# A ternary image layer: where its activations are scaled, rounded and searched for their maximum

## The reference

```python
def bitnet_linear(x, W, b):
    w_scale = jnp.maximum(jnp.mean(jnp.abs(W)), 1e-05)
    qW = jnp.sign(W) * (jnp.abs(W) > 0.5 * w_scale).astype(W.dtype)
    i_scale = jnp.maximum(jnp.max(jnp.abs(x)), 1e-08) / 127.0
    qx = jnp.clip(jnp.round(x / i_scale), -128.0, 127.0)
    out = jnp.einsum('...i,oi->...o', qx, qW) * (w_scale * i_scale)
    return out + b
vis = bitnet_linear(dinov2_features, W_d2v, b_d2v)
image_embeds = bitnet_linear(vis, W_img, b_img)
fused = bitnet_linear(text_embeddings, W_txt, b_txt)
for Wa, ba in ((W_att0, b_att0), (W_att1, b_att1)):
    kv = bitnet_linear(image_embeds, Wa, ba)
    k = jnp.concatenate([kv, kv], axis=-1)
    scores = jnp.einsum('bse,bpe->bsp', fused, k) * inv_sqrt_e
    attn = jax.nn.softmax(scores, axis=-1)
    fused = fused + 0.1 * jnp.einsum('bsp,bpe->bse', attn, k)
avg_img = jnp.mean(image_embeds, axis=1, keepdims=True)
concatenated = jnp.concatenate([fused, jnp.broadcast_to(avg_img, (b, s, e))], axis=-1)
h = jax.nn.relu(bitnet_linear(concatenated, W_f1, b_f1))
return bitnet_linear(h, W_f2, b_f2)
```

## Time and profile before

| | us |
|---|---|
| median of 3 runs (2675.1 to 2678.14) | 2677.37 |
| the profiled execution | 2671.04 |
| its span | 2669.1 |
| PE busy in the span (share) | 2413.4 (90%) |
| DVE busy (share) | 1359.3 (51%) |
| ACT busy (share) | 931.5 (35%) |
| ternary layer, from its first DMA issue to the next layer's | 1712.8 to 2111.9 |

### The profile page before, as it was taken

How to read it: one execution, slowest core, us unless ns; L and a number is a source line. 1 busy time by engine, 2 the same in 40 slices (tenths; PEclk the granted TensorE clock), 3 DMA queues, 4 the chain that set the end, 5 groups by cost and what they waited for, 6 DMA issues and landing times. The chain is left out here.

```text
span 2669.1 us, 31308 instructions
## 1 busy us (share of the span) xinstructions
PE 2413.4 (90%) x11901; PEld 1244.3 (47%) x11901; DVE 1359.3 (51%) x1929; ACT 931.5 (35%) x1903; POOL 650.8 (24%) x538
## 2 busy tenths in 40 slices
PE   7899999899999999878699799886988679999997
PEld 4454444344555555445445454354665323333332
DVE  5799999315788876630545412385444511111114
ACT  3677676025433335201122110285333212222221
POOL 0489888100000000010211000000000033444442
PEclk9999999999999999989789899998998789999998
DMA  3632222555344445315600100202000252460534
GB/s 106 250 97 92 92 86 85 125 202 207 112 169 162 163 118 171 134 53 212 213 0 0 44 1 3 97 1 95 1 1 4 103 209 100 200 279 27 234 112 158
DMA packets 97066, 301.29 MB, mean 113 GB/s; under 512 B 27114, under 2 KB 57990, under 8 KB 82332
## 3 DMA queue, kind: packets, MB, share of 16 engines
q1 hardware_dynamic: 63264, 171.06, 19.1%
q0 software_dynamic: 33664, 128.35, 13.1%
HBM read 446.13 MB, written 47.22 MB: 185 GB/s over the span
## 5 line engine op out<-in xcount | busy, mean ns | idle before, releaser
L1064 PE MATMUL psum<-at_Wv,at_context 128*128 128x512 f32 (+1 forms) x576 | 265.0, 599 | 0.0
L837 PE MATMUL psum<-mb_context,mb_key_w 128*128 128x361 f32 x768 | 252.4, 478 | 11.4 <-PEq L894 6.2
L778 DVE TENSOR_TENSOR_SCAN ms_state<-ms_decay,psum 128x800 f32<-128x800 f32 x128 | 233.0, 1820 | 6.1 <-DVE psum L775 1.7
L3134 ACT ACTIVATE tf_hidden<-psum,tf_b 128x64 f32<-128x64 f32 x512 | 108.2, 362 | 363.9 <-PE psum L3091 338.9
L3102 PE MATMUL psum<-tf_W,tf_hidden 128*64 128x512 f32 x1024 | 228.1, 597 | 3.9 <-ACT tf_hidden L3134 2.4
L3080 PE MATMUL psum<-tf_W,tf_x_T 128*64 128x512 f32 x1024 | 228.7, 597 | 1.7 <-issue 0.8
L837 PEld LDWEIGHTS psum<-mb_context,mb_key_w 128*128 128x128 f32 x768 | 141.5, 191 | 126.3 <-issue 31.5
L810 POOL TENSOR_TENSOR x_rows<-ms_state,mb_C_everywhere 128x800 f32<-128x800 f32 x86 | 161.9, 1886 | 102.7 <-DVE ms_state L778 86.5
L1165 ACT ACTIVATE mb_weights_and_rows<-psum,at_neg_max 100x722 f32<-100x722 f32 x128 | 110.4, 862 | 143.1 <-DVE at_neg_max L1227 142.9
L3015 POOL DMA_INDIRECT tf_W<-in_L_W,tt_weight_row x120 | 119.5, 996 | 164.2 <-PE psum L3080 116.6
L1227 DVE TENSOR_REDUCE at_neg_max<-psum 100x1 f32<-100x722 f32 x128 | 115.5, 903 | 78.1 <-PE psum L1085 77.7
(11 more groups left out here) (489 smaller groups left out, 3802.6 us busy)
## 6 DMA issues: line engine op xcount, KB each, us to landing
at_piece<-in_L_W_f POOLq DMA_DIRECT2D x24, 1024.0 KB, 5.9
keys_dram<-x_rows SPq DMA_DIRECT2D x128, 180.5 KB, 1.9
mb_key_w<-keys_dram SPq DMA_DIRECT2D x64, 361.0 KB, 3.2
sf_W<-in_L_W SPq DMA_DIRECT2D x16, 1024.0 KB, 7.0
tf_W<-in_L_W SPq DMA_DIRECT2D x8, 2048.0 KB, 20.9
mb_context<-in_ctxT SPq DMA_DIRECT2D x16, 541.5 KB, 4.4
at_context<-in_ctxT SPq DMA_DIRECT2D x8, 1083.0 KB, 4.9
ternary_dram<-at_piece_made POOLq DMA_DIRECT2D x14, 512.0 KB
```

Source lines behind the costliest of these rows:

```text
L778: nc.vector.tensor_tensor_scan(state[:, n % RH, :], decay[:, g % RA, :, :].rearrange("p b l -> p (b l)"), drive, 0.0, ALU.mult, ALU.add).t ...
L837: last = nc.tensor.matmul(side("key", u, t == KE - 1)[:, 0:SH], lhsT=wk[:, k, e * P:(e + 1) * P], rhs=keys[:, h, k, :], start=(k == 0), st ...
L1064: last = nc.tensor.matmul(bank[0:rows_of(t), :], lhsT=ctxT[:, b % 2, k, t * P:t * P + rows_of(t)], rhs=wv[:, k, h * BANK:(h + 1) * BANK], ...
```

## The change

Five edits. (1) Scales, bias, `d2v` weights and the first vision chunk get buffers of their own (`FirstSeen`), loaded by SyncE during the feed-forward's last product; the text maximum is taken there too, batch by batch. (2) `see` and `bl_img` become one block; the last chunk's maximum is taken in four pieces; the chain's TensorE steps stand between text units; the first chunk is rounded in halves; ScalarE's scalings stand between its drains. (3) `bl_emb` is gone: its chain stands at the start of `ternary_attend`, and VectorE scales and rounds the image embeddings there, half a chunk at a time (`quantise`), the first two chunks before the attention and the other six inside it. The weights of the last products are loaded in two parts when chunks 4 and 6 have been rounded, as they take their place. (4) `joint_linear`: the maxima over `x_cols` are taken in the odd phases of the attention, ScalarE rounds the means, VectorE rounds the first half of the text before it scales the second; the last hidden maxima are taken unit by unit. (5) In the output layer VectorE scales half of the first batch. All large buffers lie in one tensor, `tn_space`.

The cut diff:

```diff
+            for b in range(NB if most is not None else 0):
+                dve.wait_ge(turned.done(b), turned.n + b + 1)
+                nc.vector.tensor_reduce(most[:, b:b + 1], c.xT[:, :, b * L:(b + 1) * L], mybir.AxisListType.XY, ALU.max,
+                                        apply_absolute_value=True)
...
+    def load(self, sp):
+        c = self.c
+        sp.dma_start(self.scales[:, :], c.scales[:, :]).then_inc(self.loaded, 16)
+        sp.dma_start(self.w[:, :, :], made_ternary(c, "d2v")).then_inc(self.loaded, 16)
+        sp.dma_start(self.rows[:, :, :], c.vision[0].rearrange("p (k s) -> p k s", k=KC)).then_inc(self.loaded, 16)
+        sp.dma_start(self.bias[:, :], c.dram["L1_bias_cols"]).then_inc(self.loaded, 16)
...
+        TURN_AT, GIVE_AT = 4, 5
+        BY_SCALAR = {3: (5, 0), 6: (5, 1), 9: (6, 0), 12: (6, 1), 15: (7, 0), 18: (7, 1)}
...
             for v, (h, f) in enumerate(x_units):
-                u = len(units) + v
+                if v == TURN_AT:
+                    i_top.turn(pe)
+                if v == GIVE_AT:
+                    i_top.give(pe)
+                u = N + v
...
+            for f in range(KD):
+                prod.wait_free(pe, N + NX + f)
+            for h in range(2):
+                pe.wait_ge(i_rounded, h + 1)
+                for f in range(KD):
+                    last = image_half(f, 0, f, h)
+                    if h:
+                        last.then_inc(prod.filled, 1)
+            for v, (b, f) in enumerate(units):
+                if b == 0:
+                    continue
+                if f == 0:
+                    pe.wait_ge(i_rounded, b + 2)
+                prod.wait_free(pe, N + NX + v)
+                for h in range(2):
+                    last = image_half(v, b, f, h)
+                last.then_inc(prod.filled, 1)
...
+            for v, (b, f) in enumerate(units):
+                u = N + NX + v
+                prod.wait_full(act, u)
+                nc.scalar.activation(wide[:, b, f, :].rearrange("p (z s) -> p z s", s=SH), prod.bank(u), ACT.Identity,
+                                     scale=i_oscale[:, :], bias=bias_of("img")(f), accum_out=sums[:, f, b:b + 1]).then_inc(prod.done(u), 1)
+                if v in BY_SCALAR:
+                    z, h = BY_SCALAR[v]
+                    nc.scalar.activation(wide[:, z, :, part(h)], wide[:, z, :, part(h)], ACT.Copy,
+                                         scale=i_top.inv[:, :], bias=MAGIC).then_inc(i_scaled_s, 1)
...
+                for f in range(KD) if b == NB - 1 else (None,):
+                    largest(b, f, 0).then_inc(seen_most, 1)
+            dve.wait_ge(seen_most, NB - 1 + KD)
+            i_top.start(dve, amax[:, :])
+            i_top.finish(dve)
+            nc.vector.tensor_tensor(i_oscale[:, :], i_top.scale[:, :], one_scale("img"), ALU.mult).then_inc(i_scale_ready, 1)
+            dve.wait_ge(i_top.inv_ready, 1)
+            def scale(at, n):
+                nc.vector.tensor_scalar(at, at, i_top.inv[:, :], MAGIC, ALU.mult, ALU.add).then_inc(i_scaled, 1)
+                dve.wait_ge(i_scaled, n)
+            def spread(dst, at):
+                nc.vector.tensor_scalar(dst, at, MAGIC, None, ALU.subtract).then_inc(i_rounded, 1)
+            for h in range(2):
+                scale(wide[:, 0, :, part(h)], h + 1)
+                spread(seen(0, h), wide[:, 0, :, part(h)])
+            whole = lambda b: image[:, :, b * S:(b + 1) * S]
+            for b in range(1, 4):
+                scale(wide[:, b, :, :], b + 2)
+                spread(whole(b), wide[:, b, :, :])
+            largest(0, None, N + NX)
+            scale(wide[:, 4, :, :], 6)
+            spread(whole(4), wide[:, 4, :, :])
+            for b in range(5, NB):
+                dve.wait_ge(i_scaled_s, 2 * (b - 4))
+                spread(whole(b), wide[:, b, :, :])
...
+            top.start(dve, cmax[:, :])
+            top.finish(dve)
+            nc.vector.tensor_tensor(oscale[:, :], top.scale[:, :], wscale, ALU.mult).then_inc(oscale_ready, 1)
+            dve.wait_ge(top.inv_ready, 1)
+            for z in range(2):
+                nc.vector.tensor_scalar(c.xT[:, :, half(z)], c.xT[:, :, half(z)], top.inv[:, :], MAGIC, ALU.mult, ALU.add).then_inc(scaled, 1)
+                dve.wait_ge(scaled, z + 1)
+                nc.vector.tensor_scalar(catq[:, 0:KD, half(z)], c.xT[:, :, half(z)], MAGIC, None, ALU.subtract).then_inc(rounded, 1)
...
+            for lo, hi, b in f_parts:
+                sp.wait_ge(e_rounded, 2 * b + 2)
+                sp.dma_start(wf[:, lo:hi], c.ternary[:, c.ternary.shape[1] - F_ALL + lo:c.ternary.shape[1] - F_ALL + hi]).then_inc(f_loaded, 16)
...
+            def quantise(b, z):
+                if b >= NB:
+                    return
+                at = wide[:, b, :, part(z)]
+                nc.vector.tensor_scalar(at, at, e_top.inv[:, :], MAGIC, ALU.mult, ALU.add).then_inc(e_scaled, 1)
+                dve.wait_ge(e_scaled, 2 * b + z + 1)
+                nc.vector.tensor_scalar(seen(b, z), at, MAGIC, None, ALU.subtract).then_inc(e_rounded, 1)
+            e_top.start(dve, amax[:, :])
+            e_top.finish(dve)
             at0 = TERNARY.index("att0")
-            nc.vector.tensor_scalar(kscale[:, :], wscale[:, at0:at0 + 2], iscale[:, :], None, ALU.mult).then_inc(scale_ready, 1)
+            nc.vector.tensor_scalar(kscale[:, :], wscale[:, at0:at0 + 2], e_top.scale[:, :], None, ALU.mult).then_inc(scale_ready, 1)
+            dve.wait_ge(e_top.inv_ready, 1)
+            for b in range(2):
+                for z in range(2):
+                    quantise(b, z)
             nc.vector.memset(prob[:, :, S:], 0.0).then_inc(cleared, 1)
             nc.vector.memset(kr[64:P, :, :, ST - 1, :], 0.0).then_inc(cleared, 1)
+            for s in range(2):
+                query(0, s)
             dve.wait_ge(cleared, 2)
             ringR.grant(dve)
-            for s in range(2):
-                query(0, s)
-            take_rows(0, range(NR))
+            take_rows(0, range(4))
+            quantise(2, 0)
+            take_rows(0, range(4, 8))
+            quantise(2, 1)
+            take_rows(0, range(8, NR))
+            own(nc.vector.tensor_scalar(sums[:, :, :], sums[:, :, :], 1.0 / S, None, ALU.mult))
+            own(nc.vector.tensor_reduce(cmax[:, NB:], sums[:, :, :], mybir.AxisListType.XY, ALU.max, apply_absolute_value=True))
...
                     take_rows(f + 1, range(2, 4) if s == 0 else range(4, 9))
+                quantise(f + 3, 0)
+                quantise(f + 3, 1)
...
+                    else:
+                        b = f // 2 * 2 + s
+                        nc.vector.tensor_reduce(cmax[:, b:b + 1], c.xT[:, :, b * L:(b + 1) * L], mybir.AxisListType.XY, ALU.max,
+                                                apply_absolute_value=True)
```

408 lines of the change are left out of this document (207 added, 201 removed).

## The result

The changed kernel takes 2643.62 us (median of 4 runs, 2639.63 to 2648.33), the kernel before, run beside it on the same chip, 2676.23 (4 runs): ratio 0.9883, 95% interval [0.9867, 0.9898]. In the first experiment, the changed kernel again, it was 2641.02 (6 runs) against 2673.31 (8 runs): 0.9895 [0.9877, 0.9913]. The ratios are estimates of their own and not the quotients of the medians, which are 0.9878 and 0.9879.

The account below looks back on a forecast made before the run. TensorE bounds the attention, VectorE the stretches between stages. Gains of 2.7 + 3.3 + 15.3 + 4.7 + 2.4 = 28.4 us take the profiled 2671.04 to 2642.6, and the median, 6.3 above, to 2649.0; range 2642 to 2662.

Parts of the forecast that it names:

- the sum: Ternary layer: gains of 2.7, 3.3, 15.3, 4.7 and 2.4 us over five steps, 28.4 in all.
- First loads: Layer's start: four loads moved ahead, first vision matmul sooner, with VectorE's eight text maxima setting it; gain 2.7 us.
- Merged stage: Vision and image product in one block: text tail and boundary go, VectorE sets the end; gain 3.3 us.
- Rival B: Merged stage: ScalarE is the bound, drains at 1.28 plus half scalings; loss of 2.8 there, 2655 us; chance 10 in 100.
- Quantising in the attention: Image maximum's end to turning of keys: 12.5 us instead of 27.7, remaining chunks scaled inside the attention; gain 15.3.
- The cover: Attention phases: VectorE's waits for TensorE hide its halves, costed at nothing; without it 3.4 us in each of five phases.
- Rival A: Attention: VectorE is late, all ten halves uncovered, 17 us lost, 2666; half of them, 2657; chance 12 in 100.
- its neighbour: VectorE's halves run at one element a cycle, 3.2 us; gain 10, 2667; chance 3 in 100.
- The margin: Attention phases: 3.4 us of VectorE's halves fit into its 3.46 wait before the first addition, leaving 0.06.
- Joint layer's start: Attention's end to first joint matmul: 4.6 us instead of 9.26, without the maximum over the columns; gain 4.7.
- Output: Output layer: last maximum over 400 elements saves 1.25 us, first row scaled by two engines 1.2; gain 2.4.
- Rival C: Attention phases: waits for VectorE's halves keep TensorE at the lower clock, 7.7 us a phase, up to 2710; chance 2 in 100.

Follow-up runs that it names:

- three edits together: Changed kernel with text maximum cut in three, ScalarE's half scalings earlier, and chunk 1 scaled by ScalarE at the attention's start: 2633.55 us, ratio 0.9875.
- the kernel with three roundings more: Changed kernel with each half of chunks 3 to 7 rounded four times instead of once; 198.33 us from first turned key to last addition, whole time not compared.
- the last kernel: Changed kernel with three edits together plus unread matmuls keeping TensorE busy, 36 of them around the search before the first key product: 2625.45 us, ratio 0.9834.

## Why the prediction was right

The forecast was 2649.0, the time is 2643.62. The layer gained 27.4 where the sum said 28.4, so the mechanism and nearly all of the size came as worked out. The medians fell by 32.6; the other 5.2 are outside the layer, where only the early loads and maxima were added, and no cause was sought. The forecast's distance from the time so lies outside what it worked out, and the landmarks are the better test. Step by step:

1. First loads: 2.7 foreseen, 2.85 measured, and VectorE's maxima set it, as said. The second chunk was in time.
2. Merged stage: 3.3 foreseen, 3.64. The wait for ScalarE was 2.87 for 2.5, a drain 0.93 for 0.95, a half of ScalarE's 1.39 for 1.3, and VectorE's halves 1.83 for 1.7. TensorE started 2.68 after the first scaling (1761.75 to 1764.43), for 2.4. Two misses nearly cancel: the first scaling came 38.96 behind the first vision matmul for 39.8, and from it to the end of the maxima it took 49.47 for 48.9. Rival B is refuted by the drains, and by the stage getting longer without ScalarE's halves, not shorter.
3. Quantising in the attention: 15.3 foreseen (0.1 of it from no row), 14.25 measured. The first key product came as worked out (4.26, for 0.31 + 2.04 + 0.2 + 1.7), and the mis-sized term is what follows: three halves and four units, 8.3 in the sum, took 9.23. I let VectorE's halves set it, when the earlier trace rows held a row against that: 40 matmuls in 9.14, with all the data there. In the changed kernel too VectorE was not what TensorE waited for. The fourth half was rounded at 1820.90, and TensorE came to it at 1821.73, 6.25 behind the first key product for the 5.1 in the sum; the four units then took 2.98 for 3.2. Up to 1819.9 the clock was granted 0.50, with a matmul started every 0.30, and from 1821.0 on each unit started as ScalarE had finished a drain. With the data there earlier (three edits together) the stretch was no shorter; with the clock held up as well it was 7.82.
   The cover held: phases unchanged, the halves worth some 20 us elsewhere. Rival A is refuted, its neighbour too, since halves of four strided pieces run at the speed of whole chunks: 0.97 for 1444 columns, 1.72 for 2888. The margin was larger than the 0.06 that I read from the first addition's wait: another 1.9 a phase cost at most 0.17, since it went into the second addition's wait, which ended for TensorE's sake.
4. Joint layer's start: 4.7 foreseen, 5.1. The boundary and the chain of the maximum were shorter than the rows I took for them. From its first step (1998.32) to the first scaling the chain takes 1.66, for 2.04 in the sum, because its two steps on TensorE took 0.27 and 0.38 with 1.00 granted, where before they took 0.37 and 0.58 with 0.50:

```profile
1998.53 0.27 PE L2292 MATMUL psum<-ident,bl_f_most 128*1 128x128 f32 x1 [1.80 <-DVE bl_f_most L2299]
...
1999.17 0.38 PE L2296 MATMUL psum<-bl_f_top,tn_ones 1*128 1x1 f32 x2 [0.37 <-DVE bl_f_top L2304]
...
1999.98 1.05 DVE L2548 TENSOR_SCALAR x_cols<-x_cols,bl_f_inverse 128x1600 f32<-128x1600 f32 x1
```

5. Output: 1.2 of the first row came as 1.39, of which 0.31 is again the chain at the higher clock (1.97 to 1.66), which I had not foreseen; the row itself gave 1.08. Of the 1.25 for the last maximum only 0.25 is in the landmarks: VectorE's last maximum did shrink to 0.57, but the joint product before it took 46.18 instead of 45.19, as the granted clock was 0.50 for its first 5.5 us instead of its first 3.5. In steps 4 and 5 the clock so gave 0.7 and took 1.0 where the sum did not know of it; that these nearly cancel is luck.

Rival C, the clock in the phases, did not come: 1.00 in the window above. It did in the kernel with three roundings more (0.91), so it was a real danger of more work in the waits. What it had right in kind is that waits for VectorE lower TensorE's clock, at the ends of the stages and in the last phase. That was there before the change too, and I had taken TensorE's time in these places as given.

## What to carry to other kernels

Look in the bound engine's steady loop for waits of the engine that does the preparation: work moved into them was nearly free here up to their sum, and beyond it cost more than itself. Before you shorten what TensorE waits for, divide the time of the matmuls behind the wait by their number: where they ran at the lower clock, faster supply gave nothing here, and cheap matmuls in the wait gave what the supply did not. And compare kernels by stretches between landmarks, which here repeated within 0.03 us while the times of one kernel moved by more than ten.

## What the runs showed of the hardware

Behind waits for VectorE TensorE ran at the lower of its two levels (granted 0.50 to 0.69 in the windows above, 24 matmuls at 0.275 where the next 16 took 0.18), but not always: with the same waits of 1.89 and 0.38 ahead of them, the last 48 sums took 5.52, 7.0 or 8.07, depending on the kernel, and 8.07 again in the second trace of the changed one. An edit elsewhere in the layer can so move 3 us in a stage that it does not touch. What decides it stays open; that the clock does it, and that matmuls whose results nobody reads keep it up, was shown in the last phase, before the joint product and before the key products. Before the output product ten of them ran mostly at the lower level themselves (0.39 each, granted 0.62); in the last kernel six ran at 1.00, and what made the difference is open. The Trainium skill (TensorE: Matmul & The Clock Gate, HAM oscillation) tells of bursts that start at the lower clock behind waits for a DMA; the traces agree, with VectorE as what is waited for, at 6.60 us for the first 24 key products.

ScalarE's drains got longer one by one in the merged stage, from 0.95 to 1.06 (1767.78 to 1800.34), and were back at 0.95 when ScalarE began to wait for TensorE. Behind each other they started every 0.93 all the while, so the growth cost nothing; its cause was not sought.
